# Forty gathers, each with a clear behind it, ahead of the first stores, and four gathers instead of two between the later adds

## What is computed

```python
h = _L0_tok_ref(x)                                   # 32 x 938 x 128
h = h + _L0_attn_ref(_layernorm(h, axis=-1), ...)
h = h + _L0_ffn_ref(_layernorm(h, axis=-1), ...)

def _L0_ffn_ref(x, Wr, W1, b1, W2, b2):
    logits = x_flat @ Wr
    probs = jax.nn.softmax(logits, axis=0)
    vals, idx = jax.lax.top_k(probs.T, C)            # 8 experts, C = 1024
    selected = x_flat[idx]
    h = jax.nn.gelu(jnp.einsum('ecd,edf->ecf', selected, W1) + b1[:, None, :], approximate=False)
    out_e = jnp.einsum('ecf,efd->ecd', h, W2) + b2[:, None, :]
    weighted = vals[..., None] * out_e
    output = jnp.zeros_like(x_flat).at[idx.reshape(-1)].add(weighted.reshape(-1, Dd))
```

## Time and profile before

| | us |
|---|---|
| median of the timed runs | 578.6 |
| timed runs | 576.7, 578.6, 583.95 |
| span of the profiled execution | 605.3 |

### The profile page before, as it was taken

One profiled execution on the slowest core, in us unless ns is written; L12 is line 12 of the kernel. 1 busy time (PEld: TensorE's weight loads), 2 busy tenths in 40 slices (PEclk: granted clock), 3 DMA queues, 4 the chain that ended last, 5 costly groups with the idle time before them and its releaser, 6 DMA issues.

```text
span 605.3 us, 11347 instructions
## 1 busy us (share of the span) xinstructions
PE 397.3 (66%) x3577; PEld 320.0 (53%) x3577; DVE 425.8 (70%) x1653; ACT 292.2 (48%) x560; POOL 298.7 (49%) x213
## 2 busy tenths in 40 slices
PE   5798898999888889997000033210199989997900
PEld 5786788865877788764000022110057667775700
DVE  3877878898488887898888878911787658866100
ACT  2787840076699740177545500120258667686400
POOL 0467830058478730076000007776235687888774
PEclk9999999999899999999555555555579989999965
DMA  8679606699888227699999501121011344443332
GB/s 162 132 183 272 150 15 162 142 253 241 194 148 148 58 48 157 201 275 254 323 318 318 190 0 44 49 52 48 17 28 61 67 74 67 65 75 44 31 30 22
DMA packets 86116, 77.44 MB, mean 128 GB/s; under 512 B 15022, under 2 KB 82930, under 8 KB 85810
## 3 DMA queue, kind: packets, MB, share of 16 engines
q1 hardware_dynamic: 68674, 64.52, 41.6%
q0 software_dynamic: 10368, 8.40, 9.8%
q10 hardware_dynamic: 7024, 3.89, 2.7%
HBM read 52.27 MB, written 39.39 MB: 151 GB/s over the span
## 4 chain that ended last, share of the span: by engine, by line
PE 32%; DVE 21%; issue 14%; DMA 10%; POOL 10%; ACT 6%; another core or an unknown queue 5%; SPq 1%; ACTq 1%; DVEq 0%; POOLq 0%
PE banks L1003 7%; POOL out L1843 7%; PE banks L1030 5%; PE banks L929 5%; PE banks L1133 4%; PE banks L1146 4%; PE banks L1040 3%; DMA xin<-in_x 3%; ACT xn L680 2%; PE banks L915 2%; DMA ring<-toeplitz 2%; DVE xn L1512 2%; DMA const<-constants 1%; DVE xn L1576 1%
## 5 line engine op out<-in xcount | busy, mean ns | idle before, releaser
L1829 POOL DMA_INDIRECT hid<-kept,index x64 | 65.0, 1015 | 115.6 <-DVE index L1624 97.0
L1214 DVE BATCH_NORM_STATS2 stats<-hid 120x6 f32<-120x128 f32 (+1 forms) x512 | 104.9, 278 | 19.8 <-ACT hid L671 19.4
L1843 POOL DMA_INDIRECT out<-hid,index x56 | 88.6, 1582 | 25.9 <-issue 16.3
L929 PE MATMUL banks<-const,xt 128*120 128x128 f32 x512 | 74.0, 290 | 12.0 <-ACT xt L666 11.5
L775 ACT ACTIVATE xt<-banks 128x480 f32<-128x480 f32 x64 | 36.3, 570 | 84.9 <-PE banks L1030 83.7
L929 PEld LDWEIGHTS banks<-const,xt 128*120 128x120 f32 x512 | 63.9, 192 | 20.7 <-ACT xt L666 14.4
L1751 POOL TENSOR_TENSOR small<-small,powers 120x16 f32<-120x16 f32 (+2 forms) x18 | 47.9, 2662 | 47.1 <-DVE small L1232 47.1
L1819 POOL TENSOR_TENSOR small<-small,powers 120x16 f32<-120x16 f32 x15 | 43.2, 2901 | 41.7 <-DVE small L1232 36.3
L1003 PE MATMUL banks<-xn,ring 122*120 122x128 f32 x512 | 58.9, 276 | 6.3 <-DMA xn<-s 3.1
L1146 PEld LDWEIGHTS banks<-w_ring,xn 128*128 128x128 f32 x512 | 60.5, 196 | 3.9 <-issue 3.9
L1003 PEld LDWEIGHTS banks<-xn,ring 122*120 122x120 f32 x512 | 57.6, 189 | 7.4 <-issue 6.9
(11 more groups left out here) (222 smaller groups left out, 705.1 us busy)
## 6 DMA issues: line engine op xcount, KB each, us to landing
kept<-out SPq DMA_DIRECT2D x1, 15008.0 KB, 50.5
xin<-in_x SPq DMA_DIRECT2D x28, 480.0 KB, 6.9
out<-hid SPq DMA_DIRECT2D x14, 960.0 KB, 11.1
w_ring<-in_L_ffn_W SPq DMA_DIRECT2D x16, 256.0 KB
ring<-toeplitz SPq DMA_DIRECT2D x32, 112.5 KB
toeplitz<-ring SPq DMA_DIRECT2D x6, 545.0 KB, 11.3
out<-hid SPq DMA_DIRECT2D x2, 784.0 KB
xin<-in_x SPq DMA_DIRECT2D x4, 384.0 KB
```

Source lines behind the costliest of these rows:

```text
L929: mm = pe.matmul(banks[0:L, 2 + n % 4, i * D:(i + 1) * D], xt[:, n % 2, i, :], cut["basis_t"], start=True, stop=True)
L1214: ins = dve.bn_stats(stats[:, slot, b, :], hid[:, bass.ds(c * HB + b, 1), :].rearrange("p a k -> p (a k)"))
L1829: pool.indirect_dma_start(found[:, n, :], None, kept, bass.IndirectOffsetOnAxis(ap=index[:, n:n + 1], axis=0)).then_inc(found_in[e], 16)
L1843: pool.indirect_dma_start(rows, at_rows, adds[:, n, :], None, compute_op=ALU.add, oob_is_err=True, bounds_check=ROWS * FRAMES - 1).then_in ...
```

## The change

`FOUND_FIRST` goes from 54 to 40 and `FOUND_BETWEEN` from 2 to 4. Behind each of the 40 first gathers POOL clears the table `e2`; from the second on, a clear waits for the one before it.

```diff
-FOUND_FIRST = 54
+FOUND_FIRST = 40
 WEIGHED_AFTER = {3: (3, 5), 5: (5, 7), 6: (7, 8)}
-FOUND_BETWEEN = 2
+FOUND_BETWEEN = 4
...
+        paced = sem("paced")
...
+            def pause(n):
+
+                if n:
+                    pool.wait_ge(paced, n)
+                pool.memset(e2[:, :, :], 0.0).then_inc(paced, 1)
+
             pool.wait_ge(kept_in, 16)
             for n in range(FOUND_FIRST):
                 find(n)
+                pause(n)
             n = FOUND_FIRST
             for e in range(E):
                 add(e)
```

## The result

| | before | changed |
|---|---|---|
| median of the timed runs, us | 578.6 | 604.2 |
| timed runs, us | 576.7 to 583.95 | 601.5 to 605.2 |
| span of the profiled execution, us | 605.3 | 602.4 |

The changed kernel takes 1.0415 times as long, 95% interval 1.0332 to 1.0499. The forecast was 602.0 us in a range from 590 to 611. The two profiled spans would say the opposite, a gain of 2.9 us. The profiled execution of before lies 26.7 us above the median of its timed runs; that of the changed kernel was timed itself, at 604.21 us, 1.8 above its span. The experiments have to say what this is.

What follows compares the result with a forecast made beforehand. POOL's instructions were taken as the path in the last 129 us; term one +12.3 and term two +11.1 sum to +23.4 us, on the median of 578.6 giving 602.0 us, range 590 to 611.

Steps and rivals of the forecast that it cites:

- POOL as the path of the last 129 us: From expert 1's first add at 476.17 us to the end, POOL's adds and gathers are the path.
- term one: Gaps behind experts 1 to 5: five gaps of four gathers take 26.0 us instead of 13.7, +12.3 us, nothing hidden.
- term two: Expert 6's first add: last four gathers come late, so POOL waits for answer(6,0) from 578.1 to 589.2, +11.1 us.
- The clears: Behind the 40 first gathers: 0.31 us each, pairs every 1.56 us, ending at 428.7, under 431.2; cost nothing.
- The bound of 1.86 us: Upper limit for a gather and its clear, if the clear adds another 0.30 us of issue.
- rival of 610.6 us: First add of expert 0 9.5 us late if a clear costs 0.61 us: +8.6 us; chance 0.14 with clears holding up DVE.
- The first gap: Between adds of experts 0 and 1: stores and four gathers end at 447.1, under expert 1's 448.0; costs nothing.
- The idle time of DVE: 28.16 us ahead of three comparisons of `choose`, taken as a mark of the profiled execution, absent from timed runs.
- the clears give DVE its idle time back: Ahead of `choose`: timed runs have the 28.16 us and spaced gathers remove it, 573.8 us; chance 0.12.
- The clock: PE waits over 20 us for expert 7's frames, then works at half clock: +12, 614 us; chance 0.05.

Runs made afterwards that it cites:

- the second profile: The kernel before, unchanged, profiled once more: 582.9 us, span 581.1 us, beside a median of 579.3 for seven more runs on that chip.
- The same step alone: Kernel before, its ten late gathers laid out as 2, 2, 2, 0, 0, 4 behind experts 0 to 5: 616.9 us, ratio 1.019.
- both orders changed: Changed kernel with both answers of expert 6 ahead of moments_of_found(7) on DVE, and down(13) ahead of expert 7's first-half turn on PE: 602.15 us.

## Why the prediction was right, and where it was not

**POOL as the path of the last 129 us, and term one.** Right for the kernel before, and for the changed one but for the one wait that term two is about. The five gaps of four gathers take 25.6 us (forecast 26.0) and those of before, in the second profile, 13.7. Term one is +11.9 us against +12.3.

**Term two, the last four gathers.** Right in mechanism and size: without a wait POOL would have begun expert 6's adds at 548.13 + 0.95 + 0.30 = 549.4; it began at 561.27, +11.9 against +11.1. Most of the difference is the 0.9 us between the end of the answer and the start of the add, which I had at nothing. The same step alone cost 11.9 us on a chip of the other kind, and putting the last gathers ahead of expert 5's adds took the wait away. Together, terms one and two are 23.8 us, and the stretch from expert 1's first add to expert 6's is 23.5 longer. Expert 7's first add had its cover, though less of it: its answer was ready at 575.40 + 0.69 = 576.1 us, 2.3 us ahead of it, where the forecast had 3.2.

**The clears.** Right that they are covered, since without them the stretch has the same length. The size was off: I took 0.31 us each, the duration alone. A clear takes 0.33 us, but the issue ahead of the next gather falls from 0.30 to 0.17, so a pair starts every 1.44 us, not 1.56, and the cover is 5.07 us, not 2.5. The bound of 1.86 us and its rival of 610.6 us are out. The sum of that rival has a slip: by its own terms the clears start to cost from (431.2 - 362.53 - 3.8) / 40 = 1.62 us a pair, not from 1.58. Nothing rests on it.

**The first gap.** Here a step failed. I let expert 1's first add wait for DVE's answer, 85.5 us behind the first gather (448.0 - 362.53), so that nothing could be won there. In the second profile of before POOL itself is the path at this place: its first add of expert 1 starts after 87.2 us, with only issue ahead of it, and in the changed kernel after 83.5. Two numbers were off. The answer's time came from an execution with idle time in it: DVE also idled there ahead of this answer, 4.22 us with no releaser named, beyond the 28.16 that I had taken out. In both later profiles the answer is ready 80.7 us behind the first gather (444.19 + 0.69 - 364.21 and 444.59 + 0.69 - 364.61), so with 0.9 us to the add it is due at 81.6, not 85.5. And POOL in the kernel before was slower than forecast: its 54 gathers are done after 73.4 us, not 71.4, partly because without the idle time one more of them runs beside a scan of DVE (timeline of POOL in the second profile):

```profile
408.12 2.37 POOL L1829 DMA_INDIRECT hid<-kept,index  x1 [0.30 <-issue]
```

So fewer gathers in front give back 3.7 us that the sum has at 0. Against that stand 1.5 us more from expert 7's first add to the end of the span, which lie behind the last add and stay unexplained. The sum of the stretches is +20.9, not +23.4. On 578.6 us that makes 599.5, so that the median of 604.2 came within 2.2 us of the forecast is in part the luck of three runs.

**The idle time of DVE.** I took it for a mark of the profiled execution. That is wrong in its cause, and it only held for the comparison at hand because the timed runs of before were free of it. Three chips gave medians of 578.0 to 579.3 us for the kernel before, two gave 605.05 and 602.1, each in all of its timed runs. The seven profiles taken on the three faster chips, of whichever kernel, have none of it; the five taken on the two slower ones all have some, from 7 us in the changed kernel to 27.5 and more. So it goes with the chip (or with how the program was loaded there), and not with profiling. The kernel before itself was never profiled on a chip known to be slower; which chip its first profile came from isn't on record, and that it was one of these is a conclusion from its span.

**The rival "the clears give DVE its idle time back".** Wrong for the runs that were compared, and borne out in part on the slower kind of chip: the idle time ahead of `choose` is gone there, in a kernel that has both clears and 40 instead of 54 gathers in front. That the clears do it is supported by the run with 24 of them; 40 gathers without clears never ran there. Its size was wrong: for a gain of 28.16 us less 23.4, it forecast 4.8 us less than before; measured was +1.4 (606.4 against 605.05). Of the missing 6.2 us, 4.5 are at expert 1's first add, where new idle time of 7.01 us on DVE follows stores and gathers without clears. Which of the two chips one measures on decides between 4% slower and no difference.

**The clock.** In the changed kernel PE waited 23.30 us for expert 7's turn. Timeline of PE, then two stretches of it (us, busy PE, PEld, DVE, ACT, POOL, PE clock, DMA share, GB/s):

```profile
557.33 1.11 PE L1119 MATMUL banks<-const,xn 128*128 128x128 f32 x4 [23.30 <-ACT xn L830]
558.23 5.21 PE L1147 MATMUL banks<-w_ring,xn 128*128 128x128 f32 x32
```

```profile
557.00:562.00 5.00, 4.67 (x25) 4.68 (x26) 3.27 (x15) 4.95 (x9) 0.73 (x1) 0.57 0.00 0
562.00:580.00 18.00, 16.14 (x97) 11.75 (x96) 4.22 (x7) 6.30 (x11) 13.32 (x9) 1.00 0.34 31
```

The granted clock was at 0.57 in the first 5 us (mostly the lower level, 0.5 or 1.2 GHz) and 1.00 (2.4 GHz) behind them. The 32 matmuls of down(13) took 5.21 us, and in the first profile of before, at 1.00, 3.74; the turn ahead of them took 1.11 us against 0.66. answer(6,1) came 564.21 + 0.69 - 550.61 = 14.3 us behind the start of the statistics instead of 12.4, and expert 7's first answer 25.5 instead of 23.6: 1.9 us later, which is what these two rows of PE lost at the lower clock (1.47 + 0.45). answer(6,1) was there at 564.9 and the fifth add started at 568.79; covered, as forecast.

**What DVE waits for in the idle time.** The trace's semaphore events answer half of it. The semaphore by which PE tells DVE that a comparison's matmuls are done (`row_ready`) has events at 399.32, 412.64 and 425.93 us, each 0.02 us ahead of one of the three comparisons of the earlier trace rows; the matmuls that raise it had ended at 393.30, 394.37 and 401.12 us (timeline of PE in the first profile of before; the first row holds the matmuls of three halves):

```profile
391.51 2.86 PE L1107 MATMUL banks<-xin,ring 128*128 128x122 f16 x24 [0.71 <-DVE ring L1562]
...
400.13 0.99 PE L1107 MATMUL banks<-xin,ring 128*128 128x122 f16 x8 [5.75 <-issue]
```

So DVE waits for a raise that comes 6.0, 18.3 and 24.8 us late; in the second profile of before such an event stands 0.02 us or less behind the matmul. It isn't DVE alone either. In the changed kernel on the slower chip, PE had finished down(2) at 438.78 + 3.73 = 442.51 us; DVE went on at 448.59 with this, and ACT, waiting for PE's turn of 443.31 us, at 448.65 (timelines of PE and ACT):

```profile
438.78 3.73 PE L1147 MATMUL banks<-w_ring,xn 128*128 128x128 f32 x32
```

```profile
448.65 0.60 ACT L838 ACTIVATE xt<-banks 128x512 f32<-128x512 f32 x1 [3.85 <-remote]
```

That is what "remote" means in these rows: an event just before the instruction, and no instruction near it that raises the semaphore. The traces of the slower kind also lack a part of these events: 6843 to 7216 are recorded in each of the five and in the first profile of before, and 7952 to 7999 in each of the eight without idle time. So single events there are to be read with care; that the matmuls were long done when DVE started is in the rows of PE and DVE themselves.

**What stays open.** What makes the raises late. The queues show no packet but the gathers' own from 384 to 430 us, so a late fetch of code, which the rule of the Trainium skill (Runtime: NRT & Kernel Launch, Instruction fetch mechanics) would allow, is not seen, and that DVE and ACT were let go within 0.1 us of each other speaks against it too. The third pause of the earlier trace rows lasts until 425.95 us, 4.9 us beyond the end of the last gather before it (420.11 + 0.94), so a gather in progress isn't needed for it. That gathers every 1.25 us pile something up which gathers every 1.44 us let drain fits the shrinking steps with 24 clears and the return of the idle time behind them, but it is argued, not shown; nor is it shown whether the pace or the clear itself matters. Also open: 54 gathers with 40 clears never met a chip of the slower kind, nor did 40 gathers without clears; so the best layout there isn't known. Two were measured to beat the kernel before beside it there: 24 clears with the old layout, by 1.0% (0.7 to 1.4%), and, on the other chip, the changed kernel with both orders changed, by 0.4% (0.2 to 0.7%). On the faster kind nothing here beats the kernel before.

## What to carry to other kernels

Moving work of the engine that ends last from a place where it has to run anyway into its last stretch costs all of it, and a gather moved behind the work that used to hide its consumers costs, on top, what of their chain is no longer hidden: look at what stands between the last producer and the instruction that needs its result. When a profiled span and the timed runs of one kernel differ by more than a few us, look for idle time that no releaser explains, and profile again, on another chip too, before taking any due time from that trace. A cure for such idle time is worth measuring on the chips that have it and on those that don't, beside the kernel before each time.

## What the runs showed of the hardware

- The same kernel takes 578 to 579 us on three chips and 602 to 605 us on two. On such a chip, and in a profile 26.7 us too long, DVE sat idle 27.5 and 28.2 us beside indirect gathers that POOL starts every 1.25 us; the semaphore events it waited for came 6 to 25 us behind the matmuls that raise them.
- A clear of 128 x 256 words between two indirect DMAs on POOL takes 0.33 us and adds 0.19 (1.44 us from pair to pair against 1.25), since the issue ahead of the next DMA is 0.17 us instead of 0.30. With 24 of them the idle time ahead of `choose` was 7.6 us.
- A gather that starts beside DVE's scan of 128 x 960 takes as long as the scan still runs and 0.75 us more. Before, it started at 367.84 and ended at 370.68 us, the scan at 369.93; in the changed kernel it ran from 370.69 to 372.77 us, with the scan ending at 372.01 (timeline of DVE):

```profile
369.85 2.16 DVE L1577 TENSOR_TENSOR_SCAN xn<-xin,xn 128x960 f16<-128x960 f16 x1
```
